# Two stores, then two loads: a different order for SyncE's transfers in a convolution kernel

## The chip, the cores and the metric

The kernel runs on one core of one Trainium2 chip. The metric is device time in microseconds (us) for one execution. The times are the median of 3 runs; the profile is one more execution of its own.

## What is computed

The input is x, 2048 images of 64 channels and 16 by 16 pixels in float32 (134 MB); the output has the same shape. The reference, cut to what matters:

```
g = x.reshape(B, 32, 2, 16, 16)               # group norm: 2 channels a group
n = (g - mean(g)) / sqrt(var(g) + 1e-5)       # over 2 channels x 256 pixels
xp = pad(n, 1);  xp[DST] = xp[SRC]            # 30 border cells wrapped (hexagonal board)
up, left, right = three 4x4 convs of stride 2, 64 -> 64 channels, 5 taps each, + bias
out[0::2, 0::2] = up;  out[1::2, 0::2] = left;  out[1::2, 1::2] = right
return x + out * OUT_MASK
```

So each image is read once, normalised, convolved, added to itself and written once.

## The kernel before

The batch is cut into 64 chunks (NCHUNK) of 32 images. A chunk is a tile of 128 partitions (2 images x 64 channels) by 16 pairs (G) x 256 pixels: 2 MB. Its data lives in one of 8 slots of the tile xs (SLOTS): it is loaded there, normalised from there into tn, and the result of the convolution is added to it in place; then the slot is stored to the output. Slot k % 8 belongs to chunk k, so chunk k + 8 can't be loaded before chunk k has been stored.

Each engine has its own stream of instructions over the chunks, and semaphores tie them together:

- SyncE (SP) issues all transfers: `load(k)` (L167) and `store(k)` (L173). There is one queue; every load and every store goes into it in the order in which SP issues them. `store(k)` first waits for bank_added, which says that chunk k's last sum is in its slot. A load into a slot that was used before waits for the semaphore `stored` of that slot.
- VectorE (DVE) works out the statistics of chunk k + 1 (L222) in between the small steps on the moments of chunk k (L230 to L265), and then normalises half of chunk k (L270). The first L222 of a chunk waits for its load.
- ScalarE (ACT) takes the root for chunk k (L303), then moves the four banks of chunk k - 2 out of PSUM (L338), then normalises the other half of chunk k (L309).
- GpSimd (POOL) adds the four banks of chunk k - 2 onto xs (L393) and then copies the wrapped border of chunk k (L404).
- TensorE (PE) does the taps as matmuls (L449) for chunk k once its border is there, with a small matmul (L461) ahead of each pair of banks.

So at the time when DVE starts on chunk k + 1, the banks of chunk k - 2 are about to be added: three chunks lie between the load that was just used and the next store.

Loads 0 to 6 are issued ahead of the first store: 0 in four quarters, 1 and 2 after the three weights, 3 to 5 after the biases, 6 after the weights have been turned. From then on a loop over k issues `store(k)` and `load(k + 7)` in turn. Chunk 63 is stored in two halves (L205), whose sums are made last.

Of the kernel before, what the change touches and what calls it, by code (L numbers as in the profile page):

```python
# [16 lines left out]
NCHUNK = B // (2 * G)  # L17
SLOTS = 8
# [68 lines left out]
def hex_conv(nc, x, w_up, b_up, w_left, b_left, w_right, b_right, out):  # L87
    ctx = ExitStack()
    with ctx:
# [3 lines left out]
        def sem(name):  # L93
            return ctx.enter_context(nc.semaphore(name))
# [32 lines left out]
        stored = [sem(f"stored{s}") for s in range(SLOTS)]  # L127
# [35 lines left out]
        @block.sync  # L163
        def _(sp):
            def load(k):
                s = k % SLOTS
                sp.dma_start(xs[:, s, :].rearrange("p (g q) -> p g q", g=G), x_dram[k]).then_inc(loaded[s], 16)  # L167

            def store(k):

                s = k % SLOTS
                sp.wait_ge(bank_added, NB * (k + 1))
                sp.dma_start(out_dram[k], xs[:, s, :].rearrange("p (g q) -> p g q", g=G)).then_inc(stored[s], 16)  # L173

            for n in range(4):
                pairs = slice(QUARTER * n, QUARTER * (n + 1))
                sp.dma_start(xs[:, 0, :].rearrange("p (g q) -> p g q", g=G)[:, pairs],  # L177
                             x_dram[0][:, pairs]).then_inc(quarter[n] if n < 3 else loaded[0], 16)
            for t, w in enumerate((w_up, w_left, w_right)):
                sp.dma_start(raw[:, t * C * 16:(t + 1) * C * 16],  # L180
                             w.rearrange("o c a b -> o (c a b)")).then_inc(w_loaded, 16)
            load(1)
            load(2)
            for t, b in enumerate((b_up, b_left, b_right)):
                for h in range(2):
                    sp.dma_start(bias[C * h:C * h + C, t:t + 1],
                                 b.rearrange("(o a) -> o a", a=1)).then_inc(b_loaded, 16)

            for k in range(3, SLOTS - 2):
                load(k)  # L190

            sp.wait_ge(bank_empty, PREP_BANKS)
            load(SLOTS - 2)

            for k in range(NCHUNK - 1):
                store(k)
                if k == 0:
                    load(SLOTS - 1)
                elif k + SLOTS - 1 < NCHUNK:
                    sp.wait_ge(stored[(k - 1) % SLOTS], 16 * ((k - 1) // SLOTS + 1))  # L200
                    load(k + SLOTS - 1)
            for half in range(2):
                pairs = slice(G // 2 * half, G // 2 * (half + 1))
                sp.wait_ge(bank_added, NB * (NCHUNK + half))
                sp.dma_start(out_dram[NCHUNK - 1][:, pairs],  # L205
                             xs[:, SLOTS - 1, :].rearrange("p (g q) -> p g q", g=G)[:, pairs]
                             ).then_inc(stored[SLOTS - 1], 16)
            for s in range(SLOTS):
                sp.wait_ge(stored[s], 16 * (NCHUNK // SLOTS + (s == SLOTS - 1)))
# [161 lines left out]
        def _(pool):  # L371
# [26 lines left out]
            def wrap(k):  # L398

                b = k % 2  # L400
                pool.wait_ge(t_dve, k + 1)
                pool.wait_ge(t_act, k + 1)
                for dst, src, dims in WRAPS:
                    last = nc.gpsimd.tensor_copy(view(tn[b], dst, [(T_PAIR, G)] + [(d, n) for d, _, n in dims]),  # L404
                                                 view(tn[b], src, [(T_PAIR, G)] + [(d, n) for _, d, n in dims]))
                last.then_inc(t_ready, 1)
# [102 lines left out]
```

## Time and profile before

| | before |
|---|---|
| median of 3 runs | 754.72 us (754.32 to 757.72) |
| profiled execution, its own time | 756.86 us |
| span of that execution | 755.1 us |
| busy: PE / DVE / ACT / POOL | 93% / 90% / 76% / 65% |
| moved by DMA | 269.68 MB, mean 357 GB/s over the span |
| mean granted TensorE clock | 0.992 |

The span runs from the first to the last instruction; the execution's own time has 1.8 us more around it. The share of busy time is an average over the whole span. The DMA queue's time share is a sum over packets that overlap, so that it can come out a little over 1 when all 16 DMA engines are at work.

### The profile page before, as it was taken

How to read it: one execution, taken by the hardware profiler on the slowest of the kernel's cores; microseconds unless marked ns; L12 is line 12 of the kernel's file. 1: busy time of each engine (PE TensorE's matmuls, PEld its weight loads, DVE VectorE, ACT ScalarE, POOL GpSimd, SP SyncE). 2: the span in 40 equal slices, each digit the busy share in tenths (PEclk: the TensorE clock that was granted, in tenths of full speed). 3: DMA queues.
4: the chain of work that ended last, by engine and by line, in shares of the span. 5: the costliest groups of instructions: out<-in, count | busy, mean ns of one | idle time of the engine just before them, and what ended most of it. 6: DMA issues, size and time to landing. Idle time of an engine off the chain costs nothing.

```text
span 755.1 us, 36563 instructions
## 1 busy us (share of the span) xinstructions
PE 704.7 (93%) x15762; PEld 635.4 (84%) x15762; DVE 676.3 (90%) x1793; ACT 576.4 (76%) x1258; POOL 489.1 (65%) x1115
## 2 busy tenths in 40 slices
PE   0999999999999999999999999999999999999974
PEld 0888999899899989998988888898888888888864
DVE  5899999999999999989989999999999999999900
ACT  2687787778777877788787787787787787787853
POOL 1177667766776677667567567667667667667663
PEclk9999999999999999999999999999999999999996
DMA  9999999999999999999999999999999999999983
GB/s 261 328 360 378 377 382 377 368 359 369 364 367 380 366 364 365 364 357 369 363 361 370 369 375 371 366 377 366 375 372 364 378 369 372 362 379 372 357 288 121
DMA packets 265022, 269.68 MB, mean 357 GB/s; under 512 B 2640, under 2 KB 264784, under 8 KB 264976
## 3 DMA queue, kind: packets, MB, share of 16 engines
q1 hardware_dynamic: 264976, 269.23, 104.4%
q14 instruction: 37, 0.30, 0.1%
q8 instruction: 9, 0.15, 0.1%
HBM read 135.01 MB, written 134.22 MB: 357 GB/s over the span
## 4 chain that ended last, share of the span: by engine, by line
DMA 51%; PE 40%; ACT 2%; issue 2%; DVE 2%; POOL 1%; SPq 1%; POOLq 0%; ACTq 0%
PE bank L449 38%; DMA xs<-in_x 29%; DMA out<-xs 20%; DMA xs<-in_L_conv_w_right 2%; POOL xs L393 1%; ACT res L338 1%; DVE stats L222 1%; PE bank L428 1%; PE bank L461 1%; ACT tn L309 1%; SPq L173 0%; ACT xs L351 0%; SPq L177 0%; DVE m L235 0%; POOL tn L404 0%
## 5 line engine op out<-in xcount | busy, mean ns | idle before, releaser
L449 PE MATMUL bank<-tn,wts 64*64 64x192 f32 (+5 forms) x15600 | 690.3, 323 | 8.0 <-issue 8.0
L449 PEld LDWEIGHTS bank<-tn,wts 64*64 64x64 f32 x15600 | 616.1, 137 | 42.7 <-issue 8.1
L393 POOL TENSOR_TENSOR xs<-res,xs 128x192 f32<-128x192 f32 (+6 forms) x780 | 389.7, 537 | 80.1 <-ACT res L338 80.0
L222 DVE BATCH_NORM_STATS2 stats<-xs 128x6 f32<-128x512 f32 x512 | 346.9, 690 | 39.3 <-DMA xs<-in_x 39.3
L338 ACT ACTIVATE res<-bank,bias 64x512 f32<-64x512 f32 (+6 forms) x650 | 304.1, 468 | 73.1 <-PE bank L449 64.0
L309 ACT ACTIVATE tn<-xs,nmr,rstd 128x256 f32<-128x256 f32 x511 | 258.9, 592 | 5.4 <-DVE nmr L265 3.8
L404 POOL COPY tn<-tn 128x128 f32<-128x128 f32 (+2 forms) x320 | 97.9, 361 | 180.3 <-ACT tn L309 180.3
L270 DVE TENSOR_SCALAR tn<-xs,rstd,nmr 128x256 f32<-128x256 f32 x513 | 207.4, 474 | 2.3
L303 ACT ACTIVATE std<-var 128x16 f32<-128x16 f32 x64 | 13.4, 210 | 90.2 <-DVE var L243 90.2
L461 PEld LDWEIGHTS bank<-blank 128*128 128x128 f16 x130 | 12.5, 96 | 49.1 <-issue 42.0
L461 PE MATMUL bank<-blank 128*128 128x2 f16 x130 | 23.0, 177 | 15.3 <-POOL tn L404 14.4
L261 DVE SCALAR_TENSOR_TENSOR rstd<-small 128x16 f32<-128x16 f32 x64 | 31.9, 498 | 0.1
L265 DVE SCALAR_TENSOR_TENSOR nmr<-msum,rstd 128x16 f32<-128x16 f32 x64 | 26.2, 410 | 0.1
L428 PE MATMUL bank<-ident,xs 64*128 64x64 f32 x32 | 7.1, 419 | 18.6 <-ACT xs L351 18.6
L254 DVE SCALAR_TENSOR_TENSOR small<-var,small 128x16 f32<-128x16 f32 x64 | 24.4, 381 | 0.1
L258 DVE TENSOR_TENSOR small<-small 128x16 f32<-128x16 f32 x64 | 22.7, 355 | 0.1
L428 PEld LDWEIGHTS bank<-ident,xs 64*128 64x128 f32 x32 | 6.9, 329 | 18.6 <-ACT xs L351 18.6
L235 DVE TENSOR_TENSOR m<-stats,mate 128x16 f32<-128x16 f32 x64 | 19.0, 297 | 0.0
L236 DVE TENSOR_TENSOR msum<-stats,mate 128x16 f32<-128x16 f32 x64 | 17.6, 275 | 0.0
L251 DVE RECIPROCAL small<-std 128x16 f32<-128x16 f32 x64 | 14.9, 233 | 0.7 <-ACT std L303 0.7
L238 DVE SCALAR_TENSOR_TENSOR gap<-gap 128x16 f32<-128x16 f32 x64 | 14.5, 226 | 0.0
L234 DVE TENSOR_TENSOR gap<-stats,mate 128x16 f32<-128x16 f32 x64 | 13.0, 203 | 0.1
(18 smaller groups left out, 35.8 us busy)
## 6 DMA issues: line engine op xcount, KB each, us to landing
xs<-in_x SPq DMA_DIRECT2D x63, 2048.0 KB, 16.9
out<-xs SPq DMA_DIRECT2D x63, 2048.0 KB, 17.1
xs<-in_x SPq DMA_DIRECT2D x4, 512.0 KB, 5.7
out<-xs SPq DMA_DIRECT2D x2, 1024.0 KB, 5.3
xs<-in_L_conv_w_up SPq DMA_DIRECT2D x1, 256.0 KB, 8.3
xs<-in_L_conv_w_left SPq DMA_DIRECT2D x1, 256.0 KB, 9.0
xs<-in_L_conv_w_right SPq DMA_DIRECT2D x1, 256.0 KB, 11.3
bias<-in_L_conv_b_up SPq DMA_DIRECT2D x2, 0.2 KB, 7.5
```

The lines of the kernel that those rows point to most:

```text
L222: last = nc.vector.bn_stats(stats[:, k % 2, 2 * u:2 * u + 2].rearrange("p g a -> p (g a)"), both)
L254: nc.vector.scalar_tensor_tensor(small[:, 1], var[:], -0.5 / GROUP, small[:, 0], op0=ALU.mult, op1=ALU.mult).then_inc(stat_step, 1)
L258: nc.vector.tensor_tensor(small[:, 2], small[:, 1], small[:, 0], ALU.mult).then_inc(stat_step, 1)
L261: nc.vector.scalar_tensor_tensor(rstd[:], small[:, 2], 1.5, small[:, 0], op0=ALU.add, op1=ALU.mult).then_inc(stat_step, 1)
L265: nc.vector.scalar_tensor_tensor(nmr[:], msum[:], -0.5, rstd[:], op0=ALU.mult, op1=ALU.mult).then_inc(norm_ready, 1)
L270: last = nc.vector.tensor_scalar(t_image(b, g), x_image(s, g), rstd[:, g:g + 1], nmr[:, g:g + 1], ALU.mult, ALU.add)
L309: last = nc.scalar.activation(t_image(k % 2, g), x_image(k % SLOTS, g), ACT.Identity, bias=nmr[:, g:g + 1], scale=rstd[:, g:g + 1])
L338: last = nc.scalar.activation(res[onto, BANK_AT[j] + at:BANK_AT[j] + at + cols], psum[NB * b + j][banks, at:at + cols], ACT.Identity, bias ...
L393: last = nc.gpsimd.tensor_tensor(onto, view(res, at, [(rows * w, pairs), (w, rows), (1, w)]), onto, ALU.add)
L404: last = nc.gpsimd.tensor_copy(view(tn[b], dst, [(T_PAIR, G)] + [(d, n) for d, _, n in dims]), view(tn[b], src, [(T_PAIR, G)] + [(d, n) fo ...
L449: last = nc.tensor.matmul(psum[bank + j][to:to + C, at:at + cols], wts[first:first + C, NT * rect[0] + n, :], taps(b, rect, tap, g0, pairs ...
L461: nc.tensor.matmul(psum[j][:, BANK_COLS[j % NB]:BANK_COLS[j % NB] + 2], blank[:], blank[:, 0:2], start=True, stop=True, skip_group_check=True)
```

## The change

After it, SP issues two stores, `store(k)` and `store(k + 1)`, and then the two loads `load(k + 7)` and `load(k + 8)`, for k = 0, 2, 4 and so on. No transfer is added or dropped, none changes its size, its slot or its semaphore, and what each waits for is the same. The loop up to the last chunk is rewritten:

```diff
-            for k in range(NCHUNK - 1):
+            for k in range(0, NCHUNK, 2):
                 store(k)
-                if k == 0:
-                    load(SLOTS - 1)
-                elif k + SLOTS - 1 < NCHUNK:
-                    sp.wait_ge(stored[(k - 1) % SLOTS], 16 * ((k - 1) // SLOTS + 1))
-                    load(k + SLOTS - 1)
+                if k + 2 < NCHUNK:
+                    store(k + 1)
+                for n in range(k + SLOTS - 1, min(k + SLOTS + 1, NCHUNK)):
+                    if n >= SLOTS:
+                        sp.wait_ge(stored[n % SLOTS], 16 * (n // SLOTS))
+                    load(n)
```

The instructions of the other four engines stand in the same order as before. On SP, these are the first transfers of the loop: store 0, load 7, store 1, load 8, store 2, load 9, store 3, load 10 before the change.

```order
L173 DMA out<-xs 128x16x256 [waits bank_added]
L167 DMA xs<-in_x 128x16x256
L173 DMA out<-xs 128x16x256 [waits bank_added]
L167 DMA xs<-in_x 128x16x256 [waits stored0]
L173 DMA out<-xs 128x16x256 [waits bank_added]
L167 DMA xs<-in_x 128x16x256 [waits stored1]
L173 DMA out<-xs 128x16x256 [waits bank_added]
L167 DMA xs<-in_x 128x16x256 [waits stored2]
```

The same place on SP with the change, where "x2" stands for two stores that each wait for their own count of bank_added:

```order
L173 DMA out<-xs 128x16x256 [waits bank_added] x2
L167 DMA xs<-in_x 128x16x256
L167 DMA xs<-in_x 128x16x256 [waits stored0]
L173 DMA out<-xs 128x16x256 [waits bank_added] x2
L167 DMA xs<-in_x 128x16x256 [waits stored1]
L167 DMA xs<-in_x 128x16x256 [waits stored2]
```

Load 7 (and 9, 11, ..., every odd one) now stands behind one more store; the even loads stand where they stood. The second place is the end of SP's program before the change: store 55, load 62, store 56, load 63, then stores 57 to 62 and the two halves of chunk 63.

```order
L173 DMA out<-xs 128x16x256 [waits bank_added]
L167 DMA xs<-in_x 128x16x256 [waits stored6]
L173 DMA out<-xs 128x16x256 [waits bank_added]
L167 DMA xs<-in_x 128x16x256 [waits stored7]
L173 DMA out<-xs 128x16x256 [waits bank_added] x6
L205 DMA out<-xs 128x8x256 [waits bank_added] x2
```

The same place with the change (loads 61 and 62, stores 56 and 57, load 63, stores 58 to 62, the halves; their line is one further down):

```order
L167 DMA xs<-in_x 128x16x256 [waits stored5]
L167 DMA xs<-in_x 128x16x256 [waits stored6]
L173 DMA out<-xs 128x16x256 [waits bank_added] x2
L167 DMA xs<-in_x 128x16x256 [waits stored7]
L173 DMA out<-xs 128x16x256 [waits bank_added] x5
L206 DMA out<-xs 128x8x256 [waits bank_added] x2
```

Store 57 has moved from behind the last load to ahead of it.

## Rows read from the trace of the kernel before

**Rows 1.** The page: busy time, and the chain that ended last
```profile
PE 704.7 (93%) x15762; PEld 635.4 (84%) x15762; DVE 676.3 (90%) x1793; ACT 576.4 (76%) x1258; POOL 489.1 (65%) x1115
DMA 51%; PE 40%; ACT 2%; issue 2%; DVE 2%; POOL 1%; SPq 1%; POOLq 0%; ACTq 0%
```

**Rows 2.** Waits of the engines, stretch 303 to 702
```profile
engine line waited for: us in total, times, longest us
...
DVE stats L222 <- DMA xs<-in_x: 27.9, 35, 1.3
```

**Rows 3.** PE in order of time: one whole chunk, 691 to 704
```profile
691.98 5.68 PE L449 MATMUL bank<-tn,wts 64*64 64x288 f32 x100
...
697.70 5.01 PE L449 MATMUL bank<-tn,wts 64*64 64x192 f32 x140
```

**Rows 4.** Busy time, PEclk, DMA share and GB/s by stretch (us)
```profile
60.00:110.00 50.00, 50.00 (x1113) 45.11 (x1107) 49.82 (x129) 40.02 (x89) 36.24 (x80) 1.00 1.09 379
303.00:689.00 386.00, 372.81 (x8346) 335.60 (x8341) 358.29 (x955) 303.87 (x651) 258.21 (x580) 1.00 1.07 369
400.00:689.00 289.00, 276.87 (x6189) 249.04 (x6185) 269.40 (x717) 227.88 (x489) 193.93 (x436) 1.00 1.08 371
```

**Rows 5.** SP's issues in order of time, 400 to 418, and from 684
```profile
401.32 5.51 SPq L167 DMA_DIRECT2D xs<-in_x  x1
406.88 5.55 SPq L173 DMA_DIRECT2D out<-xs  x1
412.60 5.31 SPq L167 DMA_DIRECT2D xs<-in_x  x1
417.95 6.07 SPq L173 DMA_DIRECT2D out<-xs  x1
...
684.34 5.34 SPq L167 DMA_DIRECT2D xs<-in_x  x1
689.72 6.06 SPq L173 DMA_DIRECT2D out<-xs  x1
```

**Rows 6.** All 63 issues of L167: from issue to landing
```profile
DMA to landing us min/median/max: 11.2/16.9/21.6
```

**Rows 7.** SP's issues in order of time, 44 to 67: start, duration
```profile
44.66 2.84 SPq L173 DMA_DIRECT2D out<-xs  x1
47.54 5.47 SPq L167 DMA_DIRECT2D xs<-in_x  x1
55.78 3.03 SPq L173 DMA_DIRECT2D out<-xs  x1
58.85 5.50 SPq L167 DMA_DIRECT2D xs<-in_x  x1
66.55 3.17 SPq L173 DMA_DIRECT2D out<-xs  x1
```

**Rows 8.** DVE in order of time: the last load's first use
```profile
701.17 0.72 DVE L222 BATCH_NORM_STATS2 stats<-xs 128x6 f32<-128x512 f32 x1 [0.73 <-DMA xs<-in_x]
```

**Rows 9.** By stretch: only loads in the queue, only stores in it
```profile
30.00:48.00 18.00, 17.95 (x412) 16.03 (x405) 17.93 (x56) 13.22 (x29) 8.54 (x20) 1.00 1.10 349
704.00:718.00 14.00, 13.66 (x297) 12.17 (x292) 13.34 (x37) 13.65 (x30) 11.24 (x23) 1.00 1.05 350
```

**Rows 10.** By single microseconds, GB/s last
```profile
93.00:94.00 1.00, 1.00 (x32) 0.98 (x26) 1.00 (x2) 0.00 (x0) 1.00 (x2) 1.00 1.09 345
...
98.00:99.00 1.00, 1.00 (x30) 0.99 (x26) 1.00 (x5) 1.00 (x3) 0.88 (x3) 1.00 1.10 390
...
104.00:105.00 1.00, 1.00 (x26) 0.75 (x17) 1.00 (x3) 0.00 (x0) 1.00 (x3) 1.00 1.11 351
...
442.00:443.00 1.00, 0.59 (x13) 0.26 (x7) 1.00 (x4) 0.00 (x0) 0.74 (x3) 1.00 0.88 298
443.00:444.00 1.00, 1.00 (x19) 0.83 (x22) 1.00 (x4) 0.70 (x2) 0.00 (x0) 1.00 1.07 358
444.00:445.00 1.00, 1.00 (x22) 0.83 (x18) 1.00 (x3) 0.96 (x3) 0.85 (x2) 1.00 1.03 355
...
453.00:454.00 1.00, 0.71 (x10) 0.39 (x6) 1.00 (x4) 0.00 (x0) 0.99 (x4) 1.00 1.03 343
```

**Rows 11.** The issues of L173 from 40 to 60: from issue to landing
```profile
DMA to landing us min/median/max: 13.8/13.9/13.9
```

**Rows 12.** In order of time, 440 to 466: a load's first use, and adds
```profile
440.76 0.71 DVE L222 BATCH_NORM_STATS2 stats<-xs 128x6 f32<-128x512 f32 x1 [0.61 <-DMA xs<-in_x]
...
444.15 6.04 POOL L393 TENSOR_TENSOR xs<-res,xs 128x288 f32<-128x288 f32 x12 [1.41 <-ACT res L338]
```

## The prediction

> **What bounds the kernel now.** I read the busy shares first, then the chain that ended last, then the waits by stretch, then the DMA rate by stretch, and last SP's issues one by one. The busy shares point to PE, 704.7 us of a span of 755.1. The chain says otherwise: 51% of the span is DMA and 40% PE [rows 1]. The waits divide the two. From 303 to 702 us DVE waits 35 times for a load, 27.9 us in total [rows 2]; ahead of 303 (in the list from 50 to 303) no such wait stands at all. So the compute runs at its own pace first, eats up the lead that loads 0 to 6 gave it, and follows the transfers from 303 on. Its own pace is two groups of matmuls of 5.68 and 5.01 us a chunk [rows 3], about 10.8 us with the gates between them. The transfers' pace is a load and a store of 2.1 MB each at 369 to 371 GB/s [rows 4], 4.19 MB / 371 = 11.3 us a chunk, 0.5 us more than compute.
>
> The queue never runs dry. In steady state one issue follows the other on SP, each of them taking 5.3 to 6.1 us [rows 5], just what 2.1 MB takes to move at 371 GB/s (5.65 us), and each lands 16.9 us after its issue began [rows 6]: three transfers are underway, and SP is held up by a full queue, not by a semaphore. Even at the start, where SP has pauses (53.01 to 55.78, 64.35 to 66.55 [rows 7]), the rate is 379 GB/s [rows 4] and transfers lie ahead of it. So the time at which the last load lands is the DMA work that stands ahead of it divided by the rate, and the end follows at a fixed distance: chunk 63's statistics begin at 701.17 [rows 8] and the span ends at 755.1, 53.9 us of compute and last stores later.
>
> **The change, part by part.** No instruction or byte is added, so only order can cost or gain.
>
> (1) *The last load stands behind one more store.* Store 57 goes ahead of load 63. The queue is full there (issues of 5.34 and 6.06 us [rows 5]), so load 63 lands one transfer later: 5.65 us. Nothing gives it back: the 53.9 us behind it are led by compute, and one store fewer in them isn't what the end waits for. Cost +5.65 us. If the queue had slack there it would be 0; the rows show none.
>
> (2) *Loads and stores are mixed less.* The rate with only loads in the queue is 349 GB/s, with only stores 350 [rows 9]; with the two in turn it is 379 early and 371 later [rows 4]. Single microseconds show 390 in between, and drops to 345 and 351, 11 us apart, once a chunk [rows 10]. I read these drops as the moments in which all DMA engines happen to be at loads, and the rest as moments in which some are still at the store before or already at the one after, since they don't keep step. That is inference; the three rates are rows. If the surplus of 371 over 349.5, which is 21.5, is earned in the overlap near each change of direction, then half as many changes (57 instead of 113) earn half: 360.3 GB/s, 3.0% longer for the same bytes. Between the first store's landing and the last load there are 114 transfers with the change, 114 x 5.65 = 644 us, so 644 x 0.030 = +19 us. Bounds: nothing, if the surplus has another cause (0), and all of it, if pairs are enough to make every stretch pure (644 x 21.5 / 349.5 = +40 us). I take 19, since the overlap at a change has a length of its own that its distance to the next change doesn't alter.
>
> Here a rule of the Trainium skill speaks. "DMA: Bandwidth & Descriptors", section Bandwidth, gives 425 GB/s for one 16 MB load of 128 partitions, one direction only. By it a pure stretch would be no slower than a mixed one, and this term would be 0 at least. This trace has 349 GB/s over 18 us of nothing but loads [rows 9], so I go by the rows.
>
> (3) *Odd loads are issued later: do they come too late by SP's waits?* SP now stops at `store(k + 1)` with `load(k + 7)` behind it, and behind that the next stores; all other engines wait for SP only through the loads. At the start, load 7 goes out after store 1, at 55.78 + 3.03 = 58.8 instead of 47.54 [rows 7], and lands by 58.8 + 16.9 = 75.7. It is needed near 78.7: store 4 is due at 66.55 + 2 x 10.8 = 88.1, and chunk 7's statistics begin 9.4 us ahead of that (next lines). It is in time. Nor does the DMA idle: at 55.78 store 0 has been in the queue for 11.1 us, of the 13.9 that this store takes to land [rows 11]. In steady state I follow the loop: a load's first use at 440.76, the last add of the chunk three before at 444.15 + 6.04 = 450.19, 9.4 us later [rows 12]; then the second store is issued (5.6) and the load behind it lands after 16.9: 32.0 us for three chunks. The next load has already landed with it, so the fourth chunk adds compute's pace, 10.8: 42.7 us for four chunks, and the transfers take 45.2. Slack 2.5 us, so SP's waits cost nothing while the transfers are the bound. If (2) slows them, it grows. Cost 0, but this is the thin place.
>
> (4) *Fewer turnarounds.* Near where fast engines pass from a store to a load the rate falls to 298, 358 and 355 for one microsecond each, or to 343 [rows 10]. Against the 390 of an undisturbed microsecond that is (92 + 32 + 35) / 390 = 0.41 us of lost transfer in the one place and 47 / 390 = 0.12 in the other. I count nothing for it, since each store ends so whatever follows it: from 704 to 718, with stores alone, the mean is no better than 350 [rows 9].
>
> Sum: 5.65 + 19 = 24.7 us. The profiled execution's own time is 756.86; 756.9 + 24.7 = 781.5. It lies 2.1 us above the median of the runs shown, so against that median the forecast is 754.7 + 24.7 = 779.4. I say 779.
>
> **The rivals.**
> - *Only the last load matters* (mixing is worth nothing, as the page's figure has it): 754.7 + 5.65 = 760.4. For it: the slowest DMA engine may set the landing whatever the others do. Against it: 349 and 350 against 371. Chance 0.15.
> - *Faster: turnarounds cost time.* If the drops of [rows 10] belong to the change from store to load and not to the end of a store, then 28 such changes go. At 0.41 us each this is -11.4, with (1) -5.8: 749.0. It comes out faster than before only from 5.65 / 28 = 0.2 us for each change, and needs (2) to be nothing. The mean of the two places, 0.26, gives only -1.8 with (1). Chance 0.09 for faster by over 0.5%.
> - *SP's wait turns into the bound.* Should a load take longer than 16.9 + 2.5 = 19.4 us from its issue, the loop of (3) sets the pace. At 21.6, the longest seen [rows 6], it is 47.4 us for four chunks, 2.2 over; over the 14 such rounds it adds 31 us to (1): 791, and more with pure stretches on top. For it: thin slack, and every other load is asked for a chunk later. Against it: with two stores ahead of it in a queue of three transfers, the latency stays near 3 transfers. Chance 0.1.
> - *The change does nothing*, because the queue is work-conserving and the tail has slack that I don't see: within 0.5%. Chance 0.08.
>
> **How the numbers follow.** The forecast case (1) + (2) has 0.58; its own range is 766 to 795 (a third of the surplus lost, to all of it). Rival one reaches down to 760. The range from 759 to 795 leaves out the faster and unchanged cases, and the worst of the waiting case. About 0.5% (3.8 us) is what can be told from no change: slower than 758.5 are the forecast, rival one and rival three, 0.83; same 0.08; faster 0.09.
>
> **What would show it right or wrong.** Right: the rate by stretch falls to about 360 GB/s in the middle and is still 349 with loads alone; single microseconds show drops to about 350 that last 5 us and more, twice in 22 us; SP's issues still follow each other without a gap; DVE's waits for a load start well ahead of 303 and come once in two chunks, on odd chunks, some 1.5 to 2.5 us each; the last chunk's statistics begin near 726, and 54 us are left behind them. A middle that still shows 371 with the last use near 707 proves rival one. Gaps between SP's issues with a DMA share under 1 prove rival three. A rate above 375 in the middle proves the turnarounds. I would be wrong above all if the surplus of 371 over 350 isn't made by mixing but by what else differs at the two ends of the program.

## The result, and the profile after

| | before | with the change |
|---|---|---|
| median | 754.86 us (4 runs, 754.32 to 757.72) | 775.63 us (4 runs, 774.59 to 777.76) |
| ratio, 95% interval | | 1.0261 [1.0237, 1.0284] |
| profiled execution: its time / span | 756.86 / 755.1 us | 775.16 / 773.4 us |

The kernel is 2.6% slower by the ratio (19.7 us); the two medians lie 20.8 us apart. 779 us were forecast, with 759 to 795 as the range. The ratio isn't exactly that of the medians; here and below the two can differ by about 1 us. The page of the changed kernel, its busy time and chain (line numbers behind the loop are one higher than before):

```profile
PE 709.4 (92%) x15762; PEld 639.5 (83%) x15762; DVE 645.3 (83%) x1793; ACT 578.7 (75%) x1258; POOL 488.9 (63%) x1115
DMA 56%; PE 20%; DVE 5%; ACT 5%; POOL 5%; SPq 5%; issue 2%; ACTq 0%; POOLq 0%
```

PE does 5 us more than in [rows 1] in a span that is 18 us longer, and its part of the chain has fallen from 40% to 20%: the part of the program in which compute set the pace is shorter. The waits say since when. From 303 to 702 us DVE waited 27.9 us in 35 pieces before [rows 2], and none came between 702 and 720. Now, first in the stretch from 110 to 303, where it never waited before, and then from 303 to 720:

```profile
DVE stats L223 <- DMA xs<-in_x: 16.8, 6, 3.4
...
DVE stats L223 <- DMA xs<-in_x: 59.6, 18, 3.7
```

18 waits of 3.3 us instead of 35 of 0.8: they come once in two chunks, on the first load of a pair; the first of them ends at 164.92, where the kernel before had its first at 337.85. The DMA rate by stretch (stretch, its length, busy time of PE, PEld, DVE, ACT and POOL, granted clock, DMA share, GB/s), against 379 from 60 to 110 and 371 from 400 to 689 in [rows 4]:

```profile
48.00:60.00 12.00, 11.09 (x257) 9.79 (x253) 11.96 (x34) 10.26 (x22) 8.28 (x21) 1.00 0.98 335
60.00:110.00 50.00, 50.00 (x1115) 45.12 (x1111) 49.82 (x129) 40.04 (x88) 36.31 (x80) 1.00 1.08 359
110.00:303.00 193.00, 189.29 (x4245) 170.75 (x4239) 173.60 (x476) 152.78 (x328) 129.81 (x292) 0.99 1.08 363
303.00:400.00 97.00, 90.60 (x1997) 81.39 (x1992) 81.77 (x233) 71.75 (x154) 61.18 (x139) 0.98 1.07 360
400.00:689.00 289.00, 272.12 (x6040) 244.80 (x6036) 248.78 (x702) 222.86 (x477) 189.55 (x426) 0.99 1.08 362
```

The same stretches of the kernel before that were not shown yet have 375 (48 to 60), 368 (110 to 303) and 362 (303 to 400). Single microseconds of the changed kernel show of what the 362 is made:

```profile
409.00:410.00 1.00, 0.58 (x8) 0.26 (x4) 1.00 (x4) 0.58 (x2) 1.00 (x5) 1.00 1.06 356
410.00:411.00 1.00, 0.76 (x11) 0.64 (x15) 1.00 (x4) 0.96 (x3) 0.85 (x2) 1.00 1.01 247
411.00:412.00 1.00, 1.00 (x22) 0.83 (x18) 1.00 (x3) 0.97 (x2) 1.00 (x3) 1.00 0.99 308
...
416.00:417.00 1.00, 1.00 (x29) 0.99 (x31) 1.00 (x4) 1.00 (x4) 0.33 (x1) 1.00 1.11 349
...
422.00:423.00 1.00, 1.00 (x22) 0.84 (x18) 1.00 (x4) 0.22 (x2) 0.00 (x0) 1.00 1.10 348
423.00:424.00 1.00, 1.00 (x24) 0.91 (x20) 1.00 (x3) 0.97 (x2) 0.37 (x1) 1.00 1.09 386
...
430.00:431.00 1.00, 1.00 (x42) 1.00 (x36) 1.00 (x6) 1.00 (x3) 0.00 (x0) 1.00 1.09 383
...
433.00:434.00 1.00, 0.39 (x7) 0.33 (x11) 1.00 (x3) 0.97 (x3) 0.84 (x4) 1.00 1.11 306
434.00:435.00 1.00, 1.00 (x20) 0.85 (x16) 1.00 (x3) 0.96 (x3) 1.00 (x2) 0.90 0.84 229
```

One period of 23 us: a hole (247, 308) where the queue passes from stores to loads, seven microseconds in a row at 346 to 350 (416 to 423) where there had been single ones in [rows 10], then ten at 380 to 388, then the next hole (306, 229). To see which direction is the slow one, take SP's issues in steady state (start, duration) and the time from issue to landing of all 63 loads:

```profile
403.24 11.62 SPq L167 DMA_DIRECT2D xs<-in_x  x2
414.91 11.44 SPq L173 DMA_DIRECT2D out<-xs  x2
426.40 11.72 SPq L167 DMA_DIRECT2D xs<-in_x  x2
...
DMA to landing us min/median/max: 9.0/17.5/21.5
```

The two loads issued from 403.24 on land 17.7 and 17.4 us after their issues, near 420.9 and 426.6, the two stores behind them 11 to 12 us later. So the slow stretch is made of loads, and most of the ten fast microseconds behind it of stores. The rate rises at 423, 3.6 us before the second load has landed; I read this as the time by which the fastest of the 16 DMA engines is ahead of the slowest, but no record here names a packet's engine. The DMA share is 1.10 in the slow stretch and 1.09 in the fast one, so the engines are as full in both: it is the single packet of 1 KB that takes longer, about 16 x 1.10 x 1.024 / 348 = 0.052 us against 16 x 1.09 x 1.024 / 386 = 0.046 (an estimate from these rows). SP issues without a gap, 5.7 to 5.9 us each, so its new waits cost nothing there: the queue is full, it only moves less. Last, DVE's first use of the last load:

```profile
722.10 0.71 DVE L223 BATCH_NORM_STATS2 stats<-xs 128x6 f32<-128x512 f32 x1 [2.83 <-DMA xs<-in_x]
```

It comes 20.9 us later than in [rows 8]. The stretches account for this: (12 x 40 + 50 x 20 + 193 x 5 + 97 x 2 + 289 x 9) / 371 = 14.1 us for bytes that moved later, and one transfer of 5.7 us more ahead of the last load, 19.8 in all. The loss isn't spread evenly: 4.0 of the 14.1 us fall in the first 62 of these 641.

### The profile page after: what moved, and what is told of

The parts are those of the page before. It is cut to its first block, busy times and chain, and to the rows that moved or that the text cites. A ratio compares the mean times of both kernels' runs of the same rounds, so it can differ in the third digit from the quotient of the medians.

```text
span 773.4 us, 36563 instructions
## 1 busy us (share of the span) xinstructions
PE 709.4 (92%) x15762; PEld 639.5 (83%) x15762; DVE 645.3 (83%) x1793; ACT 578.7 (75%) x1258; POOL 488.9 (63%) x1115
## 4 chain that ended last, share of the span: by engine, by line
DMA 56%; PE 20%; DVE 5%; ACT 5%; POOL 5%; SPq 5%; issue 2%; ACTq 0%; POOLq 0%
DMA xs<-in_x 55%; PE bank L450 20%; POOL xs L394 5%; SPq L173 4%; DVE stats L223 4%; ACT res L339 3%; ACT tn L310 1%; DMA xs<-in_L_conv_w_right 1%; ACT wts L322 1%; PE bank L462 0%; POOL tn L405 0%; ACT xs L352 0%; DVE m L236 0%; DVE msum L237 0%; DVE var L244 0%
## 5 line engine op out<-in xcount | busy, mean ns | idle before, releaser
L271 DVE TENSOR_SCALAR tn<-xs,rstd,nmr 128x256 f32<-128x256 f32 x513 | 202.1, 463 | 2.3
L262 DVE SCALAR_TENSOR_TENSOR rstd<-small 128x16 f32<-128x16 f32 x64 | 29.2, 456 | 0.1
L255 DVE SCALAR_TENSOR_TENSOR small<-var,small 128x16 f32<-128x16 f32 x64 | 27.3, 427 | 0.1
L259 DVE TENSOR_TENSOR small<-small 128x16 f32<-128x16 f32 x64 | 16.5, 258 | 0.1
L244 DVE SCALAR_TENSOR_TENSOR var<-gap,m 128x16 f32<-128x16 f32 x64 | 14.6, 229 | 0.1
L231 DVE STREAM_SHUFFLE mate<-stats 128x48 f32<-128x48 f32 x64 | 12.8, 200 | 0.0
L236 DVE TENSOR_TENSOR m<-stats,mate 128x16 f32<-128x16 f32 x64 | 11.1, 174 | 0.0
L237 DVE TENSOR_TENSOR msum<-stats,mate 128x16 f32<-128x16 f32 x64 | 11.0, 172 | 0.0
```

The costliest lines, as they stand in the source:

```text
L255: nc.vector.scalar_tensor_tensor(small[:, 1], var[:], -0.5 / GROUP, small[:, 0], op0=ALU.mult, op1=ALU.mult).then_inc(stat_step, 1)
L262: nc.vector.scalar_tensor_tensor(rstd[:], small[:, 2], 1.5, small[:, 0], op0=ALU.add, op1=ALU.mult).then_inc(stat_step, 1)
L271: last = nc.vector.tensor_scalar(t_image(b, g), x_image(s, g), rstd[:, g:g + 1], nmr[:, g:g + 1], ALU.mult, ALU.add)
```

## The experiments

Two theories besides the prediction's were kept in view: **W**, that only SP's waits and the place of loads in the queue matter, and **T**, that a change of direction costs time. **M** is the prediction's: a queue with loads alone is slower.

### The queue by itself: copies without compute

In short (the edit is longer, and "all loads, then all stores" has a loop of its own):

```diff
-  all work of DVE, ACT, POOL and PE; weights and biases
+            for k in range(SLOTS - 1):
+                load(k)
+            for k in range(0, NCHUNK, g):          # g = 1, 2, 4
+                for m in range(k, min(k + g, NCHUNK)):
+                    sp.wait_ge(loaded[m % SLOTS], 16 * (m // SLOTS + 1))
+                    store(m)
+                for n in range(k + SLOTS - 1, min(k + SLOTS - 1 + g, NCHUNK)):
+                    if n >= SLOTS:
+                        sp.wait_ge(stored[n % SLOTS], 16 * (n // SLOTS))
+                    load(n)
```

One and one: 

> This kernel leaves out all compute: the 64 chunks are only loaded and stored again (the output is a copy of x), one store and one load in turn, seven loads ahead. It measures the DMA queue by itself. Theory M (a queue that is all loads is slower than one in which some DMA engines load while others store): 7 loads at 349 GB/s (42 us), 114 transfers mixed at 371 to 380, 7 stores: about 715 us, the one-microsecond rates as in the full kernel, 380 to 390 with a drop to about 350 once a chunk. Rival W (only the order of SP's waits mattered, the queue has one rate): about the same time for every order of transfers. Rival T (turnarounds cost): slower than the orders with longer groups.

Two and two: 

> The same copy without compute, two stores and two loads in turn. M: the middle falls to about 360 to 365 GB/s, some 15 to 20 us more than with one and one, with about 7 us of 23 at 349. W: the same time as one and one. T: 5 to 10 us faster than one and one.

Four and four: 

> The same copy without compute, four stores and four loads in turn. M: loads alone for some 18 us of 45, the surplus from mixing halves again, some 8 to 10 us more than with two and two. W: no difference. T: faster again, by 3 to 5 us.

All loads, then all stores: 

> No compute, and the stores read what the last loads left in the slots (so the output is not the copy): all 64 loads, then all 64 stores. It measures the two rates with one direction alone. M: loads at 349 GB/s, 385 us; stores somewhere from 350 (the tail of the kernel before) to 385 (the middle of a pair of stores in the changed kernel), 349 to 383 us; in total 734 to 768. W: 268 MB at the rate of the other orders. T: the fastest of all, with one turnaround.

Measured, one execution each, 717.4, 729.8, 756.2 and 783.3 us. The steps between them, 12 to 27 us, are large against the 4.6 us by which executions of one kernel here differ at most. The stretches show the rates (no other engine has work; granted clock, DMA share and GB/s stand last), one and one first:

```profile
60.00:670.00 610.00, 0.00 (x0) 1.00 1.09 380
```

Two and two, the whole middle and then three pieces of one period:

```profile
60.00:670.00 610.00, 0.00 (x0) 1.00 1.09 372
400.00:404.00 4.00, 0.00 (x0) 1.00 1.10 348
405.00:418.00 13.00, 0.00 (x0) 1.00 1.09 386
421.00:426.00 5.00, 0.00 (x0) 1.00 1.10 348
```

Four and four:

```profile
60.00:670.00 610.00, 0.00 (x0) 1.00 1.08 358
405.00:418.00 13.00, 0.00 (x0) 1.00 1.10 348
420.00:432.00 12.00, 0.00 (x0) 1.00 1.09 386
434.00:439.00 5.00, 0.00 (x0) 1.00 1.06 366
440.00:441.00 1.00, 0.00 (x0) 1.00 0.93 214
```

Loads alone, then stores alone (between the two, from 388 to 389, nothing moved, since the stores wait for the last loads):

```profile
20.00:370.00 350.00, 0.00 (x0) 1.00 1.10 348
400.00:750.00 350.00, 0.00 (x0) 1.00 1.04 343
```

The order alone sets the time, against W; and longer groups are slower, never faster, against T as the only cause. Loads alone run at 348 whether for 4 us or for 350. Two and two loses 12 us to one and one, the size of what the change loses by rate.

By size three of the four expectations missed. Two and two was to lose 15 to 20 us with 360 to 365 GB/s in the middle; it lost 12.4, with 372. Four and four was to lose 8 to 10 us more; it lost 26.4. Loads and stores apart were to take 734 to 768 us; they took 783. The first fits a queue that is slow only where all is loads: two and two has some 8 slow microseconds in 22.6, (8 x 348 + 14.6 x 386) / 22.6 = 372.5. Four and four shows that this isn't all: its stores fall from 386 to 366 after 15 us (433), and from 439 to 444, where they end, single microseconds have 313, 214, 324, 326 and 284 GB/s. From 60 to 670 us its microseconds under 340 GB/s lack 16.8 us of transfer against 386; one and one and two and two have no such microsecond.

### Which place of the last load counts

One store ahead of it and nothing else:

```diff
-                elif k + SLOTS - 1 < NCHUNK:
+                elif k + SLOTS - 1 < NCHUNK - 1:
                     sp.wait_ge(stored[(k - 1) % SLOTS], 16 * ((k - 1) // SLOTS + 1))
                     load(k + SLOTS - 1)
+                elif k + SLOTS - 1 == NCHUNK:
+                    sp.wait_ge(stored[(k - 2) % SLOTS], 16 * ((k - 2) // SLOTS + 1))
+                    load(NCHUNK - 1)
```

> The kernel before with one thing changed: store 57 goes ahead of load 63, everything else in turn as before. Theory of the prediction: 754.8 + 5.65 = 760.4 us, the last chunk's statistics begin near 706.8, the middle stays at 369 to 371 GB/s. Rival (the tail gives it back): 754 to 756 us.

Measured 761.3 us against 757.1 for the kernel before on the same chip, ratio 1.0067 [1.0040, 1.0093]: +5.1 us by the ratio (3.0 to 7.0 by its interval), +4.2 by the medians, where 5.65 were expected. DVE in order of time:

```profile
707.97 0.71 DVE L225 BATCH_NORM_STATS2 stats<-xs 128x6 f32<-128x512 f32 x1 [6.74 <-DMA xs<-in_x]
```

It waits 6.74 us for this load and starts 6.8 us later than in [rows 8], but the span is only 4.3 us longer (759.4): 51.4 us are left behind it, not 53.9. The end moves with the load, though not by all of it. Pairs, shifted by one chunk:

```diff
+            store(0)
+            refill(SLOTS - 1)                      # wait for the slot's store, then load
+            for k in range(1, NCHUNK - 1, 2):
                 store(k)
+                store(k + 1)
+                for n in range(k + SLOTS - 1, min(k + SLOTS + 1, NCHUNK)):
+                    refill(n)
```

> The change with its pairs shifted by one chunk (store 0, load 7, then stores 1 and 2, loads 8 and 9, and so on), so that load 63 goes out behind store 56 as before the change, while loads and stores are in pairs as in the change. Theory of the prediction (one store more ahead of the last load costs 5.7 to 5.9 us, the rest is the lower rate of the queue): 770 us, middle at 362 GB/s. Rival (nothing but pairing counts, the place of the last load is covered by the tail): 775 to 776 us.

Measured 776.7 us, ratio 1.0265 [1.0228, 1.0302], the same as the change: a miss. Here load 62 is the first of the last pair. DVE's last wait in this run is for that load, and none follows for load 63:

```profile
711.60 0.70 DVE L227 BATCH_NORM_STATS2 stats<-xs 128x6 f32<-128x512 f32 x1 [3.32 <-DMA xs<-in_x]
```

Chunk 62 starts at 711.60 and chunk 63 only at 721.44, when compute has got there, though its load lands one transfer behind load 62. So with pairs it isn't the last load that counts but the first load of the last pair, plus compute's pace. (In the change itself load 63 stands alone behind two stores, and is the first of its group.) Seen so, one transfer is lost in either place. To test that, the change with its end in turn again, so that load 62 too comes a store earlier (the dots stand for the pairs up to k = 52):

```diff
+            ...
+                for m in ((k, k + 1) if k >= 54 else ()):      # pairs only for k < 54
+                    if m < NCHUNK - 1:
+                        store(m)
+                    n = m + SLOTS - 1
+                    if n < NCHUNK:
+                        sp.wait_ge(stored[n % SLOTS], 16 * (n // SLOTS))
+                        load(n)
```

> The change, but the last six transfers ahead of the tail in turn again (store 54, load 61, store 55, load 62, store 56, load 63). So the last load has one store fewer ahead of it and the load before it lands a store earlier. Theory (one transfer of delay for the last load, 5.7 us; the shifted pairs showed no gain because there load 62 lands with load 63 right behind it, and compute needs 10.8 us between the two): 775.6 - 5.7 = 770 us. Rival (the last load's place doesn't matter at all once transfers are in pairs): 775 to 776 us.

Measured 772.6 us, ratio 1.0217 [1.0195, 1.0239]. Against the change's 1.0261 that is -3.3 us; 5.7 were expected, and by the ends of the two intervals it can be from nothing to 6.7. The last load is used at 718.44, 3.7 us ahead of the change. The direction is as expected, the size is less sure. So that pairs cost one transfer in either place is supported, not shown to the microsecond.

### How the loss is spread

Pairs for stores 0 to 27 only, then in turn (the same edit with 28 for 54):

> Pairs for stores 0 to 27 and their loads only, then in turn as before. Theory of the mixed queue: the loss is spread over the transfers, 15 us over 57 chunks, so 28 of them cost 7.4 us, and the last load stands where it stood: 762 us, with 359 to 362 GB/s up to about 370 us and 369 to 371 behind it. Rival (compute alone runs the first part, transfers have slack there, so that half costs nothing): 755 us. Rival (the loss is in waits that build up, not in the queue's rate): under 760 us with the rate unchanged.

Measured 766.3 us, ratio 1.0137 [1.0115, 1.0158], +10.3 us; 7.4 were expected, and by the interval it is 8.7 to 11.9, so the expectation missed. Both rivals are out: the part that compute alone had led costs full price, and more than its half. Much of that is lost early: from 48 to 60 and from 60 to 110 this run has 325 and 358 GB/s against 375 and 379, (12 x 50 + 50 x 21) / 371 = 4.4 us. Its rates, as the page's row of 40 slices (19 us each) has them:

```profile
GB/s 246 337 341 326 370 373 369 369 366 351 366 356 372 354 357 366 362 363 366 354 353 364 373 359 368 369 370 369 374 375 367 376 367 375 370 376 370 360 285 156
```

Up to the 20th, some 380 us, it has the rates of the change (326 in the fourth slice, 351 to 373 behind), and from the 25th to the 37th those of the kernel before, 367 to 376. A gain of lead that is missed early is missed for good, since the transfers are the bound at the end and nothing later catches up.

### Four and four in the full kernel

```diff
+            for k in range(0, NCHUNK - 1, 4):
+                for m in range(k, min(k + 4, NCHUNK - 1)):
+                    store(m)
+                for n in range(k + SLOTS - 1, min(k + SLOTS - 1 + 4, NCHUNK)):
                     if n >= SLOTS:
                         sp.wait_ge(stored[n % SLOTS], 16 * (n // SLOTS))
                     load(n)
```

> Four stores, then four loads. Theory of the mixed queue: if only the rate of the queue counted, about 783 to 790 us (4.4 times 3 us of last-load delay, 17 us, on top of 754.8, and 18 to 25 us for the rate). Rival (late loads by SP's order become the bound): the first load of a group is asked for after the store three chunks later than before; slack of 13 us is passed, SP shows gaps, the DMA share falls under 1 and the time goes over 820 us.

Measured 923.0 us, ratio 1.221 [1.2176, 1.2245]. Now W's mechanism is there. SP in order of time, and DVE:

```profile
409.24 0.37 SPq L173 DMA_DIRECT2D out<-xs  x1
409.66 20.60 SPq L167 DMA_DIRECT2D xs<-in_x  x4
432.93 10.15 SPq L173 DMA_DIRECT2D out<-xs  x2
```

```profile
424.33 0.70 DVE L222 BATCH_NORM_STATS2 stats<-xs 128x6 f32<-128x512 f32 x1 [15.21 <-DMA xs<-in_x]
```

A store that is issued in 0.37 us meets a queue with room, and from 406 to 410 nothing moved at all:

```profile
406.00:408.00 2.00, 2.00 (x40) 1.74 (x36) 2.00 (x6) 1.92 (x6) 1.35 (x4) 1.00 0.00 0
408.00:410.00 2.00, 2.00 (x50) 1.96 (x42) 1.12 (x5) 2.00 (x5) 1.21 (x4) 1.00 0.00 0
```

The loop of the prediction's part (3) predicts where this starts: with pairs there were 2.5 us of slack, and four and four asks for loads two chunks later still. The change stays on the good side, with no gap between SP's issues in steady state.

### The other way: halves and quarters

Each transfer cut in P parts by pairs of images, with a semaphore for each part of a slot (in short; P is 2 or 4):

```diff
+            for k in range(NCHUNK - 1):
+                n = k + SLOTS - 1
+                sp.wait_ge(bank_added, NB * (k + 1))
+                for h in range(P):
+                    put(k, h)                      # 1/P of store k
+                    fill(n, h)                     # wait for part h of the slot, 1/P of load n
```

Halves: 

> The other way: each 2 MB store and load is cut in two halves of 1 MB and these go in turn (half a store, half a load, and so on), with a semaphore for each half of a slot. Theory of the mixed queue: DMA engines that are 3 to 4 us apart never all load at once when a half takes 2.8 us, so the drops to 349 go; the middle rises from 371 to 378 or so, -10 us, 745 us. Rival (a change from store to load has its own cost of 0.2 to 0.4 us, as the drops to 298 and 343 GB/s suggest): twice as many changes cost 64 times 0.26 = 17 us, 765 to 772 us. Between the two lies 755: both, evened out.

Quarters: 

> As the run with halves, but cut in four: a quarter of a store (512 KB), a quarter of a load, in turn, a semaphore for each. Theory: halves are already shorter than the 3 to 4 us by which DMA engines are apart, so quarters add nothing: 745 to 750 us. Rival (each change of direction or each further transfer costs 0.1 us or more): 192 more changes than with halves in the store direction alone, over 765 us.

The control, with `put(k, 0)`, `put(k, 1)`, `fill(n, 0)`, `fill(n, 1)`: 

> A control for the run with halves: the same cut in halves of 1 MB with the same semaphores, but both halves of the store, then both of the load, so that the directions change as often as before. If the gain of 1.1% with halves comes from the mixing, this stays at 754 to 756 us and the drops to 349 GB/s are back. If it comes from the cut itself (a slot's first half is free earlier, a queue that holds more): 747 to 749 us.

| | median | ratio to before |
|---|---|---|
| halves in turn | 748.0 us | 0.9886 [0.9859, 0.9912] |
| quarters in turn | 749.4 us | 0.9909 [0.9892, 0.9927] |
| halves in blocks (control) | 761.0 us | 1.0064 [1.0044, 1.0084] |

Halves in turn beat both kernels: the one before by 1.1% (9 us), the change by 3.8% (28 us). The page's rates by slice (18.6 us) with halves, and two single microseconds:

```profile
GB/s 251 330 360 385 384 385 385 379 377 367 372 361 373 370 372 370 374 374 376 370 372 367 373 373 375 376 371 366 370 371 368 378 372 374 372 374 370 369 284 174
...
93.00:94.00 1.00, 1.00 (x42) 1.00 (x38) 1.00 (x4) 0.97 (x2) 1.00 (x3) 1.00 1.09 386
...
104.00:105.00 1.00, 1.00 (x44) 1.00 (x39) 1.00 (x5) 0.97 (x2) 1.00 (x4) 1.00 1.08 382
```

From the fourth to the seventh slice it is 384 to 385, where the kernel before had 378, 377, 382 and 377. The two microseconds had 345 and 351 in [rows 10], and from 86 to 130 no microsecond of the halves is under 379. In the control the drops are back, once a chunk:

```profile
93.00:94.00 1.00, 1.00 (x46) 1.00 (x42) 1.00 (x3) 0.99 (x2) 1.00 (x5) 1.00 1.10 347
102.00:103.00 1.00, 1.00 (x32) 1.00 (x34) 1.00 (x4) 1.00 (x4) 0.00 (x0) 1.00 1.02 358
```

But the middle did not rise to the 378 that was expected. Halves in turn, and then the control, have there

```profile
400.00:689.00 289.00, 282.94 (x6326) 254.88 (x6322) 272.00 (x723) 229.71 (x493) 195.38 (x440) 1.00 1.07 372
400.00:689.00 289.00, 274.80 (x6124) 247.23 (x6120) 265.12 (x710) 225.65 (x482) 192.32 (x431) 1.00 1.07 368
```

against 371 before: holes stay there with halves too (308 GB/s from 440 to 441, 297 from 462 to 463). Of the 6.4 us by which the last load is used earlier (694.78), nearly all is won ahead of 400: 385 against 379 from 60 to 110, 373 against 368 to 303, 372 against 362 to 400. The time came out near what was expected, the place of the gain did not. The other 2.8 us of the span are won behind the last load (51.1 us instead of 53.9; see "The end" below).

The control says that the cut as such doesn't help, it costs 0.6%, so the directions in turn are worth 1.8% here (1.0064 - 0.9886), 13 us. Quarters bring nothing beyond halves, as expected. The control's own loss was not expected; its last load is used at 705.42, 4.2 us late, and I haven't tested why.

## Why the prediction was right, step by step

- *What bounds.* Right. The last load's use moved by 20.9 us and the span by 18.3; SP issues back to back before and after in steady state.
- *(1) One store more ahead of the last load, +5.65.* Right in size: +5.1 us alone by the ratio, 4.2 by the medians, though the load itself came 6.8 us later. It was told too narrowly. The shifted pairs have load 63 where it was and lose as much, since then the first load of the last pair sets the end. As I read it, pairs cost one transfer wherever they are put.
- *(2) Less mixing, +19.* Right in mechanism, too large. The stretches give 14.1 us, and 371 fell to 362 rather than 360.3. What failed is the pair of end rates. I took 350 for stores alone from the program's last stretch [rows 9]; behind loads they run at 380 to 388 in the change and at 386 in the copy with two and two. So only loads have a slow stretch. A sum that has only this: 7 us at 348 instead of some 2 x 1.3 (the two drops in 22 us of [rows 10] with their edges) is 4.4 x (1 - 348/386) = 0.43 us in 22.6, 12 us for 28 pairs. The rest of the 14.1 are the first stores (next point) and the holes of (4). A count over all single microseconds from 400 to 670 says the same: those from 340 to 352 GB/s are 15 before and 65 with the change, and lack 1.5 and 6.3 us of transfer against 386.
  That 360.3 came so near to 362 is luck in part. The rule behind it, half the changes of direction earn half the surplus, fails in the copies: one and one has 380 over some 346 for one direction, half of that surplus would give two and two 363, and it has 372. In the kernel the slower loads alone would have made it less; the holes of (4) add the rest.
- *(3) SP's waits, 0.* Right in steady state, wrong at the start. I wrote that the DMA doesn't idle when load 7 comes behind store 1, and went by the time at which store 0 lands. The bytes are moved before that. Three single microseconds of the changed kernel:

```profile
54.00:55.00 1.00, 1.00 (x24) 0.91 (x20) 1.00 (x4) 0.97 (x3) 0.74 (x2) 1.00 1.07 375
55.00:56.00 1.00, 1.00 (x30) 1.00 (x25) 1.00 (x5) 1.00 (x3) 0.84 (x3) 1.00 0.70 248
56.00:57.00 1.00, 1.00 (x24) 0.75 (x15) 1.00 (x7) 1.00 (x3) 0.00 (x0) 1.00 0.36 126
```

  The queue had all but run dry (the DMA share is 0.70 and 0.36); (375 - 248 + 375 - 126) / 375 = 1.0 us is lost. The kernel before has 370 and 384 there. A second gap follows from 62 to 65, 219, 227 and 279 GB/s where the kernel before has 385 in the mean, another 1.1 us; whether it comes of the late issue or is a hole as in (4) was not tried.
- *(4) Turnarounds, 0.* Their number halved, and each hole grew. Against 385 GB/s, one hole in 23 us lacks 138 + 77 = 215 (410 to 412) or 79 + 156 = 235 (433 to 435); before there were two, of 87 + 27 + 30 = 144 and 42 against the same 385 [rows 10], 186 together. So there was nothing to win, and something to lose: from 400 to 670 the microseconds under 340 lack 4.2 us of transfer before and 7.2 with the change. The copies with one and one and with two and two have the same changes of direction, and from 60 to 670 no microsecond below 340. What makes the holes is therefore the compute beside them or the state of the queue, not the change alone. Compute isn't needed for one: four and four has 214 without it. What sets them off is open.
- *The end.* Taken as a fixed distance, which it isn't: 51.3 us from the last load's use to the end, 53.9 before. It is 51.4 with the late last load and 51.1 with halves, where the stores of the end are in their old order, and 53.7 in the control. The granted TensorE clock, which is at 2.4 GHz or at half of that, explains part of it. Before, it is 0.67 and 0.65 in the mean from 735 to 740 and to 745, after PE stood idle for 4.2 us, with two groups of matmuls still to do: 5 x 0.33 + 5 x 0.35 = 3.4 us of full speed lost. With the change it is 1.00 up to 755, then 0.66 for 5 us behind an idle 2.3 us: 1.7 us lost.

```profile
755.00:760.00 5.00, 4.92 (x117) 4.70 (x116) 0.00 (x0) 2.44 (x8) 1.95 (x7) 0.66 0.41 136
```

- *The signs.* The middle at 362, loads alone at 349 (30 to 48), SP without gaps in steady state and waits on every second chunk came as said. The slow stretch comes once in 23 us, not twice, since stores are fast; the waits are 3.3 us, not 1.5 to 2.5; the last use is at 722, not 726.
- *The range.* Its ends don't follow from the working. A third of the surplus lost gives 754.7 + 5.65 + 12.7 = 773.0, not 766, and all of it 754.7 + 5.65 + 40 = 800, not 795. The 775.6 measured lies inside either.
- *The rivals.* "Only the last load matters" gives 760.4 and is the run with that edit alone, 761.3 against 757.1; the change is well beyond, and "the change does nothing" is out with it. "Faster by fewer turnarounds" fell with the copies. "SP's wait turns into the bound" is real one size further, at four and four. The figure of 425 GB/s that the Trainium skill gives for one load of 16 MB ("DMA: Bandwidth & Descriptors", section Bandwidth) isn't reached here: loads of 2 MB, one behind the other, move at 348 GB/s over 350 us, with no compute beside them. No run here has a transfer of 16 MB.

## What to carry to other kernels

If the DMA queue is full all the time, ask of a new order what it does to the mix of directions in it and what stands ahead of the last load, before asking what it does to waits: here the queue in turn moved 380 GB/s with no compute beside it, in pairs 372, with loads alone 348. Where loads and stores are equal in bytes, try them in turn in smaller pieces: 1 MB won 1.1% here, most of it ahead of 400 us, and 0.5 MB gave nothing more. That pieces should be short against the time by which the DMA engines are apart is my reading, not shown. A transfer that lands late isn't a queue that is full: whether DMA idles is read from GB/s by the microsecond, not from the time to landing.

## What was unexpected of the hardware

- The two directions differ. Loads alone move at 348 GB/s, from the start and for as long as was tried (350 us). Stores moved at 386 for 12 us behind loads (four and four, 420 to 432), then at 366 (434 to 439), and at 343 in a run of 64 stores that began with an empty queue. Why stores alone have two rates was not tried.
- Cutting the transfers of the kernel in halves without a new order cost 0.6%, some 5 us, with 120 more transfers. The cause was not tried.
- With compute beside it, the same one-and-one order moved 371 where the copy moved 380. From 400 to 670 this is 7.2 us of transfer, and the microseconds under 340 GB/s, which the copy hasn't, make 4.2 of them.
